# Numbers and weights of all expert slots loaded at once, ahead of the slots, in a decoder layer with routed experts

## What is computed

```python
logits = jnp.einsum('bsd,ed->bse', x, router_w)
probs = jax.nn.softmax(logits, axis=-1)
topk_vals, topk_idx = jax.lax.top_k(probs, 2)
...
for eid in range(8):
    w = jnp.sum(jnp.where(idx == eid, vals, 0), axis=-1)
    h = jax.nn.gelu(x_flat @ w1[eid].T, approximate=False)     # 256 -> 1024
    y = h @ w2[eid].T                                          # 1024 -> 256
    out = out + w[:, None] * y
x = layernorm(x + out)
```

## Time and profile before

| | us |
|---|---|
| three runs | 927.92, 930.38, 937.87 |
| median | 930.38 |
| span of the profiled execution | 939.3 |
| stretch of the expert slots in it, first transposes to last matmul | 580.7 to 913.3 |
| PE busy in the whole span | 711.5 (76%) |
| DVE, ACT, POOL busy in the whole span | 377.1, 326.8, 215.8 |

### The profile page before, as it was taken

The page is one execution under the profiler, slowest core; times in us unless marked ns, Lnnn a source line. Parts: engine busy times, 40 slices in busy tenths (PEclk is TensorE's granted clock), DMA queues, the critical chain, the costliest instruction groups (busy, mean ns, idle before and its releaser), DMA issues.

```text
span 939.3 us, 13839 instructions
## 1 busy us (share of the span) xinstructions
PE 711.5 (76%) x4099; PEld 452.6 (48%) x4100; DVE 377.1 (40%) x790; ACT 326.8 (35%) x541; POOL 215.8 (23%) x265
## 2 busy tenths in 40 slices
PE   7473239999999876647888722898899898998980
PEld 3232102222222355422226622887788787887870
DVE  2153237888886366635327850111111111111113
ACT  3121226667767533323542110323222322223212
POOL 1021100111111112121110573222332233223332
PEclk9786678999999997857769955999999999999995
DMA  6999990000003407688238343111111111111105
GB/s 210 121 167 166 167 113 2 2 1 1 1 1 122 96 2 135 101 120 141 95 131 272 91 121 121 19 26 29 31 23 23 28 28 30 22 28 29 21 10 179
DMA packets 67342, 71.08 MB, mean 76 GB/s; under 512 B 14548, under 2 KB 60141, under 8 KB 67310
## 3 DMA queue, kind: packets, MB, share of 16 engines
q1 hardware_dynamic: 54574, 58.03, 31.7%
q0 software_dynamic: 8512, 8.44, 5.6%
q10 hardware_dynamic: 4224, 4.19, 1.6%
HBM read 50.45 MB, written 21.40 MB: 76 GB/s over the span
## 4 chain that ended last, share of the span: by engine, by line
PE 39%; DMA 30%; issue 8%; DVE 8%; SPq 6%; POOL 5%; ACT 2%; POOLq 1%; DVEq 0%; ACTq 0%
DMA acc<-yw,mt 12%; PE ps L1313 7%; DMA scrq<-parts 7%; PE ps L1322 6%; DMA mt<-metas 5%; PE ps L1258 5%; PE ps L1603 4%; PE ps L1592 4%; SPq L397 3%; DMA qst<-mT 3%; PE ps L1406 2%; POOL metas L665 2%; PE ps L1479 2%; POOL xt L694 2%; PE ps L1472 2%
## 5 line engine op out<-in xcount | busy, mean ns | idle before, releaser
L903 DVE TENSOR_REDUCE nmx<-ps 128x1 f32<-128x512 f32 x256 | 160.4, 683 | 55.7 <-PE ps L1258 55.7
L750 ACT ACTIVATE probs<-ps 128x512 f32<-128x512 f32 x256 | 133.6, 608 | 94.5 <-PE ps L1313 94.4
L1603 PE MATMUL ps<-wexp,hidT 128*128 x624 | 144.3, 384 | 17.6 <-ACT hidT L856 12.3
L1592 PEld LDWEIGHTS ps<-xtT,w1c 128*128 128x128 f32 x1248 | 147.7, 195 | 4.3 <-DVE w1c L363 1.5
L1592 PE MATMUL ps<-xtT,w1c 128*128 128x128 f32 x1248 | 148.2, 278 | 1.8 <-ACT xtT L850 1.8
L1603 PEld LDWEIGHTS ps<-wexp,hidT 128*128 128x128 f32 x624 | 115.4, 190 | 39.7 <-issue 25.5
L1214 DVE TENSOR_SCALAR yw<-ps,mt 128x256 f32<-128x256 f32 x39 | 18.9, 484 | 259.2 <-PE ps L1603 259.2
L1313 PE MATMUL ps<-qst,kst 99*128 (+1 forms) x256 | 95.9, 394 | 35.4 <-DMA qst<-mT 33.4
L1258 PE MATMUL ps<-kst,qst 96*128 (+1 forms) x256 | 93.9, 393 | 33.7 <-DVE nmx L903 17.2
L856 ACT ACTIVATE hidT<-ps 128x1024 f32<-128x1024 f32 x39 | 39.9, 1024 | 221.1 <-PE ps L1592 221.1
L694 POOL DMA_INDIRECT xt<-x2d,mt x39 | 43.3, 1110 | 209.7 <-DVE yw L1214 150.4
(11 more groups left out here) (166 smaller groups left out, 696.6 us busy)
## 6 DMA issues: line engine op xcount, KB each, us to landing
wexp<-in_w1T SPq DMA_DIRECT2D x8, 1024.0 KB, 5.0
wexp<-in_w2T SPq DMA_DIRECT2D x8, 1024.0 KB, 8.4
qst<-scrq SPq DMA_DIRECT2D x24, 256.0 KB, 9.4
kst<-scrk SPq DMA_DIRECT2D x24, 256.0 KB, 19.8
qst<-scr_q SPq DMA_DIRECT2D x24, 256.0 KB, 8.5
scrq<-parts SPq DMA_DIRECT2D x4, 768.0 KB, 18.4
scrk<-parts SPq DMA_DIRECT2D x4, 768.0 KB, 18.9
scr_q<-parts SPq DMA_DIRECT2D x4, 768.0 KB, 3.4
```

Source lines behind the costliest of these rows:

```text
L750: act.activation(probs[n % 8][:, :], ps[:, 4 + n % 3, :], ACT.Exp).then_inc(s_exp, 1)
L903: dve.tensor_reduce(nmx[j % 2][:, k:k + 1], ps[:, slot, :], AX.X, ALU.max, negate=True).then_inc(s_mfree, 1)
L1592: mm = pe.matmul(ps[:, 2 * (j % 2) + f // 4, f % 4 * P:(f % 4 + 1) * P], w1c[j % 2][:, k * FF + f * P:k * FF + (f + 1) * P], xtT[j % 2][:, ...
L1603: mm = pe.matmul(ps[:, 4 + j % 2, 0:D], hidT[j % 2][:, f * P:(f + 1) * P], wexp[:, ds(e * EW + KD * FF + f * D, D)], start=(f == 0), stop= ...
```

## The change

`mt` becomes one place of 2 x 39 columns, two for each slot, so no slot's numbers overwrite another's. SP loads the numbers of slots 0 to 3, then expert 7's weights, then the numbers of slots 4 to 38, one DMA each as before, without waiting for a scatter. Instead of one semaphore for each of four buffers there is one for each of three groups of slots (0 to 3, 4 to 7, 8 to 38), and it is waited for in full: GpSimd waits for all loads of a group ahead of the gather of its first slot, and DVE, which did not wait for these loads before, ahead of its work for the first slot. GpSimd's and DVE's loops are written out slot by slot; SP's too. TensorE and ACT keep theirs and are unchanged.

```diff
+META_GROUPS = ((0, 4), (4, 8), (8, NSLOT))
...
-    mt = [sb(f"mt{i}", 2, F32, R_O) for i in range(4)]
+    mt = sb("mt", 2 * NSLOT, F32, R_O)
...
-    s_mt = [sem(f"meta_loaded_{n}") for n in range(4)]
+    s_mt = [sem(f"meta_loaded_{n}") for n in range(len(META_GROUPS))]
...
+    def slot_meta(t, c):
+        return mt[:, 2 * t + c:2 * t + c + 1]
...
-        def load_meta(t, j):
+        def load_meta(t, group):
             row = sp.value_load(plan[1][0:1, ds(t, 1)], min_val=0, max_val=PAD_BLOCK * P)
-            sp.dma_start(mt[j][:, :], metas[ds(row, P), :]).then_inc(s_mt[j], 16)
-
-        for t in range(4):
-            load_meta(t, t)
-        load_expert(NE - 1)
-        with sp.Fori(0, NSLOT // 4 - 1) as i:
-            for j in range(4):
-                sp.wait_ge(s_sc, 16 * (4 * i + j + 1))
-                load_meta(4 * i + j + 4, j)
-        for t in range(NSLOT // 4 * 4, NSLOT):
-            sp.wait_ge(s_sc, 16 * (t - 3))
-            load_meta(t, t % 4)
+            sp.dma_start(mt[:, 2 * t:2 * t + 2], metas[ds(row, P), :]).then_inc(s_mt[group], 16)
+
+        for group, (lo, hi) in enumerate(META_GROUPS):
+            for t in range(lo, hi):
+                load_meta(t, group)
+            if group == 0:
+                load_expert(NE - 1)
...
-        def gather(t, j, turn):
-            pool.wait_ge(s_mt[j % 4], 16 * (turn + 1))
-            if not (isinstance(t, int) and t < 2):
+        def gather(t):
+            for group, (lo, hi) in enumerate(META_GROUPS):
+                if t == lo:
+                    pool.wait_ge(s_mt[group], 16 * (hi - lo))
+            if t >= 2:
                 pool.wait_ge(s_tpx, t - 1)
...
         for t in range(3):
-            gather(t, t, 0)
-        for t in range(4):
-            gather(t + 3, t + 3, (t + 3) // 4)
-            scatter(t, t)
-        with pool.Fori(1, NSLOT // 4) as i:
-            for j in range(4):
-                gather(4 * i + j + 3, j + 3, i + (j + 3) // 4)
-                scatter(4 * i + j, j)
-        for t in range(NSLOT // 4 * 4, NSLOT):
+            gather(t)
+        for t in range(NSLOT):
             if t + 3 < NSLOT:
-                gather(t + 3, t + 3, (t + 3) // 4)
-            scatter(t, t)
+                gather(t + 3)
+            scatter(t)
...
-        for t in range(4):
-            w1_half(t + 2, t)
-            weigh(t, t)
-        with dve.Fori(1, NSLOT // 4) as i:
-            for j in range(4):
-                w1_half(4 * i + j + 2, j)
-                weigh(4 * i + j, j)
-        for t in range(NSLOT // 4 * 4, NSLOT):
-            if t + 2 < NSLOT:
-                w1_half(t + 2, t)
-            weigh(t, t)
+        for group, (lo, hi) in enumerate(META_GROUPS):
+            dve.wait_ge(s_mt[group], 16 * (hi - lo))
+            for t in range(lo, hi):
+                if t + 2 < NSLOT:
+                    w1_half(t + 2, t)
+                weigh(t)
```

More of the change, by code:

```diff
@@ L688, in checked, with scatter @@
             return dict(bounds_check=last_row, oob_is_err=False)
-        def gather(t, j, turn):
-            pool.wait_ge(s_mt[j % 4], 16 * (turn + 1))
-            if not (isinstance(t, int) and t < 2):
+        def gather(t):
[3 more added lines that the diff above has]
+            if t >= 2:
                 pool.wait_ge(s_tpx, t - 1)
[L694 to L698, removed]
+            pool.indirect_dma_start(xt[t % 2][:, :], None, x2d,
+                                    bass.IndirectOffsetOnAxis(slot_meta(t, 0).bitcast(U32), 0),
+                                    **checked()).then_inc(s_g[t % 2], 16)
+        def scatter(t):
             pool.wait_ge(s_yw, t + 1)
-            pool.wait_ge(s_sc, 16 * t)
-            pool.indirect_dma_start(acc, bass.IndirectOffsetOnAxis(mt[j % 4][:, 0:1].bitcast(U32), 0),
-                                    yw[j % 2][:, :], None, **checked(),
+            if t > 0:
+                pool.wait_ge(s_sc, 16 * t)
+            pool.indirect_dma_start(acc, bass.IndirectOffsetOnAxis(slot_meta(t, 0).bitcast(U32), 0),
+                                    yw[t % 2][:, :], None, **checked(),
                                     compute_op=ALU.add).then_inc(s_sc, 16)
@@ L1208, in w1_half, with weigh @@
             copy_w1(dve, dve.tensor_copy, t, j, 0)
-        def weigh(t, j):
+        def weigh(t):
             dve.wait_ge(s_mm2, t + 1)
-            if not (isinstance(t, int) and t < 2):
+            if t >= 2:
                 dve.wait_ge(s_sc, 16 * (t - 1))
-            dve.tensor_scalar(yw[j % 2][:, :], ps[:, 4 + j % 2, 0:D], mt[j % 4][:, 1:2], None, ALU.mult).then_inc(s_yw, 1)
+            dve.tensor_scalar(yw[t % 2][:, :], ps[:, 4 + t % 2, 0:D], slot_meta(t, 1), None, ALU.mult).then_inc(s_yw, 1)
         dve.wait_ge(s_planned, 1)
```

## The result

The changed kernel takes 894.82 us (median of 4 runs, 888.72 to 900.84) against 930.59 us before (median of 4, 927.92 to 937.87): a ratio of 0.959, 95% interval 0.953 to 0.966. The profiled execution's span is 895.4 us against 939.3 us, 43.9 us less. The prediction said 891.5 us, 883 to 906.

The account below looks back on a forecast made before the run. The scatter-to-scatter loop, 8.55 us a slot, was taken as the bound, just longer than TensorE's work. 45.0 us gained less 6.1 us lost gives 38.9 us off the 930.4 us median: 891.5 us, range 883 to 906.

Parts of the forecast that it names:

- The loop scatter, numbers, gather sets the pace: In the expert slots, the chain from scatter to next scatter takes 8.55 us, which is the slot's period.
- 45.0 us gained at 7.24 us a slot, in the Fori loop too: Slot 3's to slot 38's hidden layer: 298.45 us falls to 253.4 us with TensorE as the only bound.
- The sequencer's lead: In TensorE's loop, its sequencer reaches the gather's semaphore 1.9 us before the hidden layer ends.
- Gathers at +3.4 us behind the hidden layer's start, nobody late: In the slots, gathers issue right behind the previous scatter and land at +6.2 us, 4.6 us to spare.
- 6.1 us lost at the start: Slot 0's gather waits for four loads, 3.4 us, and falls into expert 7's weights, 2.7 us.
- The weights' part: At the start, slot 0's gather meets expert 7's 2 MB load and lands 2.5 to 3.0 us later.
- 35 loads and two group waits at nothing: SP's loads behind expert 7's weights take 1.13 us each; waits for groups 1 and 2 are covered, no cost.
- (b): In the loop, TensorE's sequencer does not keep ahead, or part of the wait is left: 911.5 or 901 us, 15%.
- (c): Gather of slot k+3 still ends with the scatter of slot k-1 on GpSimd's queue: if late, 936.5 us, 3%.
- (e): TensorE at work without a hole for 250 us is not granted its full clock: 917 us, 3%.
- (d): One wait for 31 loads: SP's pace holds up slot 8's gather; 937 us at 3 us a load, 4%.
- costs twice: In the slots before the change, a late gather costs in front of the transposes and behind them, 0.97 instead of 0.22 us.

Follow-up runs that it names:

- experiment 3: Changed kernel with slot 0 and slot 1 as groups of their own: 886.2 us; separately, expert 7's weights loaded behind all 39 loads of numbers: 893.0 us.
- Experiment 5: Changed kernel's written-out code with four buffers for the numbers, plus TensorE's expert-number read ahead of the gather's semaphore: 924.0 us, ratio 0.990.

## Why the prediction was right, step by step

- *The loop scatter, numbers, gather sets the pace.* Right: it comes back with four buffers (8.42 us) and goes with five (7.245 us).
- *45.0 us gained at 7.24 us a slot, in the Fori loop too.* 44.88 us. The sequencer's lead was the argument. In the trace of after it stands at the gather's semaphore at 744.8 in the slot whose hidden layer starts at 743.26, 2.0 us ahead of its end, as in the earlier trace rows; this row is line 1568, the same wait:

```profile
L1568 PEldq EVENT_SEMAPHORE  x1: 51/51/51, 744.8 to 744.8; - x1
```

- *Gathers at +3.4 us behind the hidden layer's start, nobody late.* 710.40 - 707.03 (hidden layer of that slot) = 3.4 us; none of the 35 was waited for.
- *6.1 us lost at the start.* 6.97 us up to the first transposes, of which 0.18 us is the last scatter of numbers and 6.8 us the change's. The wait for three loads was 3.4 us expected and 3.36 us found (3.3 us by experiment 3). The weights' part was 2.7 us expected and 3.42 us found (3.5 us by experiment 3): this term was made too small. The gather of slot 0 landed in 6.35 us, longer than the 5.4 and 5.9 us that the range was made from the earlier trace rows. By the Trainium skill's rule that the DMA engines take turns between queues ("DMA: Bandwidth & Descriptors", "Queues, rings and completion order") this part should have been near nothing; both experiments of the start speak against using it so here.
- *35 loads and two group waits at nothing.* Right. From the first to the last of SP's 35 loads it was 38.9 us, 1.14 us each (1.13 expected).
- *The sum.* 38.9 us expected; 37.9 us from the two stretches that the change touches (44.88 - 6.97), 35.8 us between the medians, whose single runs spread over 10 to 12 us. One step failed and did little harm: that the median would stay 9 us under the profiled span. The span was forecast at 900.4 us and is 895.4 us, the median at 891.5 us and is 894.82 us, so the distance fell to 0.6 us. Of this, 5.87 us lie in the first row of the table above, ahead of everything that was forecast. So at least this part of the distance was not longer DMA latencies in the slots. Without the first row the forecast of the span would have been 894.5 us.
- Of the rivals, (b), (c) and (e) did not occur; (d) is real, and the third group stayed clear of it by 15 us (landed at about 615, asked for at 631).
- One thing in the working was said too strongly: that a late gather "costs twice". Experiment 5, on the four-buffer kernel with the same loop, shows that most of the second hole cost nothing, since the loop and not TensorE set the pace. The sum did not rest on it.

## What to carry to other kernels

Where an engine is 90% busy and still shows short waits at every turn, follow the chain once round, from a transfer to the same transfer of the next turn, and compare its length with the engine's work: if the loop is the longer, one more buffer for the thing that waits may be enough (here a fifth one of 1 KB brought all that 39 did). When small loads are gathered under one semaphore, count who waits for the first of them: here the first gather's wait for four, and its landing in a 2 MB load, gave back 7 us of 45. And before turning two instructions round on a queue, write down what each of them waits for through the other engines; the loop that this closed cost 159 us.

## What the runs showed of the hardware

- A gather of 128 rows of 1 KB, issued from GpSimd while SP's 2 MB load kept the DMA engines busy, landed in 5.4 to 6.4 us instead of 2.9 us. With small loads of 1 KB before and behind it on SP's queue (39 in all), and the 2 MB moved behind them, it landed in 2.88 us.
- TensorE kept its full clock for 254 us of work without a hole. With a hole of 2.7 us ahead of the transposes and one of 0.3 to 0.5 us behind them in each slot, the granted clock was 0.81 on average and most slots took 13.3 to 13.7 us; with the hole of 2.7 us alone it was 0.98, at 10.2 us a slot. Behind one hole of 9 us the transposes and the first 3 us of the expert output ran at the half level (0.50, 1.2 GHz), and the clock was full again 5 us behind the hole.
- TensorE's sequencer works 1.9 to 2.0 us ahead of the matmuls here, and the slots then show no trace of the 0.3 us register read and the semaphores between transposes and expert output: they are 0.21 us apart in the changed kernel, and 0.97 us apart in a slot of the kernel before whose gather was late.
